# Scatters, router gathers and the last batch moved in the experts' block of a graph transformer layer

## The reference

```python
xn = layernorm(x)
x  = x + gnn(xn, edges) + linear_attention(xn)       # gnn: mean of xn[src] by dst, a matmul, a norm
x2 = layernorm(x)
h  = (x2 @ W_gat).reshape(M, 4, 4)                   # heads, experts
e  = leaky_relu(a_src[src] + a_dst[dst], 0.2)        # a_* = (h * att_*).sum(-1), one per head
alpha = exp(e - segment_max(e, dst)) / segment_sum(...)
agg = segment_sum(h[src] * alpha, dst) + b_gat
scores = layernorm(agg).reshape(M, 4, 4).mean(1)
gate = softmax of the best two scores, 0 for the others
out = x + sum over experts of gate * (gelu(x2 @ W1 + b1) @ W2 + b2)
```

## Time and profile before

| | us |
|---|---|
| Median of three timed runs | 4273.77 |
| Profiled execution, its span (no other time of it is given) | 5331.2 |
| Set-up, to the first gather | 130 |
| Graph block, first gather to last | 2511 |
| Graph block, what is left after the gathers | 192 |
| Experts' block, all tiles | 2128 |
| Experts' block, gates and sums | 370 |

### The profile page before, as it was taken

The page is one execution under the profiler, slowest core; times in us unless marked ns, Lnnn a source line. Parts: engine busy times, 40 slices in busy tenths (PEclk is TensorE's granted clock), DMA queues, the critical chain, the costliest instruction groups (busy, mean ns, idle before and its releaser), DMA issues. The chain is left out here.

```text
span 5331.2 us, 46344 instructions
## 1 busy us (share of the span) xinstructions
PE 3564.3 (67%) x12937; PEld 2313.0 (43%) x12938; DVE 2082.9 (39%) x4892; ACT 801.1 (15%) x1970; POOL 2832.6 (53%) x2937
## 2 busy tenths in 40 slices
PE   0688888888757777777626377768685777789200
PEld 0455555555445455555413154444453454455100
DVE  5456655665546555544311020211111120212378
ACT  5111211111101111111101011111111111112000
POOL 2666666666666666666655623653636444630420
PEclk9889899998878888888767588888787788899655
DMA  7444444444445555555512111211112111211387
GB/s 250 128 109 115 112 111 112 112 115 112 112 111 148 138 153 154 162 152 152 125 33 61 18 49 28 58 38 48 35 50 43 44 48 36 60 50 48 118 254 253
DMA packets 381413, 540.57 MB, mean 101 GB/s; under 512 B 120314, under 2 KB 297818, under 8 KB 381143
## 3 DMA queue, kind: packets, MB, share of 16 engines
q0 software_dynamic: 119136, 234.44, 20.0%
q1 hardware_dynamic: 243119, 288.12, 16.8%
q10 hardware_dynamic: 19016, 16.48, 0.9%
HBM read 392.03 MB, written 146.74 MB: 101 GB/s over the span
## 5 line engine op out<-in xcount | busy, mean ns | idle before, releaser
L788 POOL DMA_INDIRECT rows<-xn_rows,gsrc x1664 | 1606.6, 965 | 908.5 <-issue 459.8
L1357 POOL DMA_INDIRECT nb<-route_rows,idx x1024 | 1000.3, 977 | 897.7 <-DVE msg L1432 480.9
L1093 PE MATMUL PS<-rows,oh 128*128 128x257 f32 x3328 | 910.0, 427 | 351.9 <-issue 220.0
L1686 PE MATMUL PS<-arena,hid 128*125 128x256 f32 x3200 | 865.1, 422 | 408.5 <-issue 298.6
L1686 PEld LDWEIGHTS PS<-arena,hid 128*125 128x125 f32 x3200 | 662.9, 209 | 621.3 <-issue 502.6
L1093 PEld LDWEIGHTS PS<-rows,oh 128*128 128x128 f32 x3328 | 693.8, 214 | 488.8 <-issue 296.6
L1621 DVE TENSOR_TENSOR y_sb<-PS,b_b 125x512 f32<-125x512 f32 x200 | 128.7, 685 | 1781.4 <-remote 975.2
L1678 PE MATMUL PS<-x2g,arena 128*128 128x500 f32 x1600 | 722.6, 610 | 147.3 <-issue 94.0
L1678 PEld LDWEIGHTS PS<-x2g,arena 128*128 128x128 f32 x1600 | 313.5, 197 | 541.6 <-issue 473.0
L1647 ACT ACTIVATE hid<-PS,b_sb 128x500 f32<-128x500 f32 x400 | 269.9, 677 | 1109.9 <-PE PS L1678 688.9
L1165 PE MATMUL PS<-own_w,p_t 128*125 128x512 f32 x400 | 231.2, 662 | 77.7 <-ACT s_t L1053 54.5
(11 more groups left out here) (304 smaller groups left out, 3086.8 us busy)
## 6 DMA issues: line engine op xcount, KB each, us to landing
y_rows<-y_sb SPq DMA_DIRECT2D x100, 512.0 KB
arena<-y_rows SPq DMA_DIRECT2D x100, 512.0 KB
rows<-xn_rows,gsrc POOLq DMA_INDIRECT x1664
nb<-route_rows,idx POOLq DMA_INDIRECT x1024
sum_rows<-kept SPq DMA_DIRECT2D x104, 128.5 KB
x_rows<-x SPq DMA_DIRECT2D x100, 128.0 KB
hid<-x_rows SPq DMA_DIRECT2D x100, 128.0 KB
m_in<-sum_rows SPq DMA_DIRECT2D x100, 125.5 KB
```

The lines of the kernel that those rows point to most:

```text
L788: pool.indirect_dma_start(out=rows[w][h][:, q, 0:D], out_offset=None, in_=xn_rows, in_offset=bass.IndirectOffsetOnAxis(ap=gsrc[:, s * HU + ...
L1093: last = mm(SUM[:, 0:D + 1], oh[w][h][:, q, :], rows[w][h][:, q, :], start=h == 0 and q == 0, stop=h == 1 and q == HU - 1)
L1357: pool.indirect_dma_start(out=nb[b % NBUF][:, c, :], out_offset=None, in_=route_rows, in_offset=bass.IndirectOffsetOnAxis(ap=idx[:, b * W ...
L1686: last = mm(Y[j % 2][e // 2][0:NP, (e % 2) * D:(e % 2 + 1) * D], hid[:, 4 * e + k, j * NP:(j + 1) * NP], w2_sb[:, e, k, :], start=k == 0, ...
```

## The change

The hundred scatters leave the graph block and stand at the head of GpSimd's queue in the experts' block, without waits. `start_ad`'s load moves in SyncE's queue from ahead of all tiles to behind the store of tile 6. The full stops (REST) go; the wait for the gather four before stays. The batches stand behind tiles 12, 20, 24, 32, 36, 41, 48, 53, 60, 65, 72, 76, 84, 88 and 96, and batch 15 (`LATE`) behind all tiles, on VectorE, ScalarE and SyncE. The joining of the lanes follows it, and TensorE's transposes for it stand behind its last tile.

```diff
 def unit_after(b):
-    t = int((b + 1) * 5.65) + 3
+    t = int((b + 1) * 5.8) + 7
     return t if t % 4 < 2 else t + 4 - t % 4
...
 # graph block, gpsimd
-                for t in range(NT):
-                    pool.wait_ge(s_hc, t + 2)
-                    pool.indirect_dma_start(out=ad_rows, out_offset=bass.IndirectOffsetOnAxis(ap=start_i[:, t:t + 1], axis=0),
-                                            in_=ad_all[:, t, :], in_offset=None).then_inc(s_ads, 16)
...
 # experts' block
-            LAST = unit_after(NB - 1)
+            LATE = [b for b in range(NB) if unit_after(b) > NT - 4]
...
 # sync
+                def store_records(b):
+                    sp.wait_ge(s_rec, b + 1)
+                    sp.dma_start(rec_rows[0:EF, :].rearrange("(p f) c -> p f c", p=P)[:, b * W:(b + 1) * W, :],
+                                 rec[b % 2][:]).then_inc(s_recs[b % 2], 16)
                 load_group(0)
                 load_group(1)
-                sp.wait_ge(s_ads, 16 * NT)
-                sp.dma_start(ad[:], ad_rows[0:EF, :].rearrange("(p f) h -> p f h", p=P)).then_inc(s_adl, 16)
                 for t in range(NT):
                     sp.wait_ge(s_yc, t + 1)
                     sp.dma_start(y_rows[t], y_sb[t % 2][:]).then_inc(s_ys[t % 2], 16)
+                    if t == unit_after(0) - 6:
+                        sp.wait_ge(s_ads, 16 * NT)
+                        sp.dma_start(ad[:], ad_rows[0:EF, :].rearrange("(p f) h -> p f h", p=P)).then_inc(s_adl, 16)
                     for b in batches_after(t - 2):
-                        sp.wait_ge(s_rec, b + 1)
...
+                        store_records(b)
...
                 for t in range(YR):
                     final_loads(t)
+                for b in LATE:
+                    store_records(b)
                 for t in range(YR, NT):
                     final_loads(t)
 # gpsimd
+                for t in range(NT):
+                    pool.indirect_dma_start(out=ad_rows, out_offset=bass.IndirectOffsetOnAxis(ap=start_i[:, t:t + 1], axis=0),
+                                            in_=ad_all[:, t, :], in_offset=None).then_inc(s_ads, 16)
                 for b in range(NB):
                     if b >= NBUF:
                         pool.wait_ge(s_nbf, b - NBUF + 1)
                     for c in range(W):
-                        if (b or c) and c % REST == 0:
-                            for q in range(AHEAD):
-                                pool.wait_ge(s_nb[q], (b * W + c) // AHEAD * 16)
-                        elif b or c >= AHEAD:
+                        if b or c >= AHEAD:
                             pool.wait_ge(s_nb[c % AHEAD], (b * W + c) // AHEAD * 16)
 # vector, behind the loop over tiles
-                    for part, at in ((lane_ends, 1), (over_lanes, 2), (lane_sums, 3), (first_maxima, 4), (first_records, 5)):
-                        if t == LAST + at:
-                            part()
+                for b in LATE:
+                    scores(b)
+                    records(b)
+                for part in (lane_ends, over_lanes, lane_sums, first_maxima, first_records):
+                    part()
 # scalar, behind the loop over groups
-                    if g == LAST // 4:
-                        act.wait_ge(s_endd, 1)
-                        a(dc[:], dc[:], ACT.Exp).then_inc(s_ende, 1)
+                for b in LATE:
+                    act.wait_ge(s_dif, b + 1)
+                    a(dd[:], dd[:], ACT.Exp).then_inc(s_ex, 1)
+                act.wait_ge(s_endd, 1)
+                a(dc[:], dc[:], ACT.Exp).then_inc(s_ende, 1)
 # tensor: the waits and transposes of the lanes' ends (before, inside group() behind tiles LAST + 2 and
 # LAST + 3) stand, unchanged and in the same order, behind the last group
```

More of the change, by code:

```diff
@@ L50 @@
 AHEAD = 4
-REST = 16
 EVEN = 112
@@ L1287, in build @@
             batches_after = lambda t: [b for b in range(NB) if unit_after(b) == t]
-            LAST = unit_after(NB - 1)
-            assert LAST + 4 < NT and LAST // 4 == NG - 2
+            LATE = [b for b in range(NB) if unit_after(b) > NT - 4]
             @block.sync
@@ L1310, in _ @@
                     sp.dma_start(y_rows[t], y_sb[t % 2][:]).then_inc(s_ys[t % 2], 16)
+                    if t == unit_after(0) - 6:
+                        sp.wait_ge(s_ads, 16 * NT)
+                        sp.dma_start(ad[:], ad_rows[0:EF, :].rearrange("(p f) h -> p f h", p=P)).then_inc(s_adl, 16)
                     for b in batches_after(t - 2):
-                        sp.wait_ge(s_rec, b + 1)
-                        sp.dma_start(rec_rows[0:EF, :].rearrange("(p f) c -> p f c", p=P)[:, b * W:(b + 1) * W, :],
-                                     rec[b % 2][:]).then_inc(s_recs[b % 2], 16)
+                        store_records(b)
                     if t % 4 == 0 and t // 4 + 2 < NG:
@@ L1688, in group @@
                         last.then_inc(s_y, 1)
[L1689 to L1698, removed]
                 for g in range(2):
@@ L1706, in _ @@
                     group(g, g % 2, g // 2)
+                pe.wait_ge(s_ends, 1)
+                for k in range(4):
+                    last = nc.tensor.transpose(HP[0][0:20, k * P:(k + 1) * P], ends[:, k, :], ident)
+                last.then_inc(s_endt, 1)
+                pe.wait_ge(s_endc, 1)
+                pe.wait_ge(s_fx, 1)
+                nc.tensor.transpose(HP[1][:, 0:20], fm[:, 0:P], ident[0:20, 0:20])
+                nc.tensor.transpose(HP[1][:, 20:40], fx[:, 0:P], ident[0:20, 0:20]).then_inc(s_back, 1)
 _INS = ["x", "src", "dst", "L0_gnn_weight", "L0_gnn_bias", "L0_mix_Wqkv", "kv_turned", "out_turned", "L0_mix_bout",
```

## The result

The kernel after takes **4129.98 us** (median of four runs, 4125.64 to 4134.59) against 4273.77: a ratio of **0.9667** [0.9655, 0.9679], 3.3% or 144 us less. Forecast were 4184 us (2.1%) and a range of 4113 to 4305. The side was right, the size was not.

The account below looks back on a forecast made before the run. GpSimd was taken to set the graph block's step, and the experts' loop in timed runs; in the profile it alternated with TensorE. Profile -110 + 0 + 32 = -78 and timed -77 - 30 = -107 gave -90: 4184 us, range 4113 to 4305.

Parts of the forecast that it names:

- Post steps: Graph block's end: twelve or thirteen steps remain after the last gather, 4.6 us each, 60 us, plus some 8 for last sums.
- timed view: Sum for a run without most of TensorE's slowdown: graph tail -77 us, experts' block 1494 to 1464, together -107.
- profile's -110: Graph block, by the 5331.2 us profile: without scatters its last step ends near 2710 for 2820.25 us.
- Scatters at the head: Start of the experts' block: 100 scatters of 1.27 us add 127 us to GpSimd; SyncE's wait taken as 0.
- Full stops: Router's gathers: 63 stops, 13 on a wait for `records`, the other 50 cost 2.3 us each; removal saves GpSimd 113 us.
- Loop over tiles: 0: Experts' block, in the profile's terms: the loop of about 2128 us does not change.
- The chain of the last batch: End of the experts' block: 57 us from the last tile to the weighing against 25 before, +32 us.
- The final sum: Whole kernel: -78 us by the profile, -107 in a timed run, forecast -90, giving 4184 us.
- Stops as relief: Rival, experts' block: stops relieve TensorE, so without them it crawls more; slower, 4347 us, chance 0.13.
- Timed runs bound by TensorE: Rival, experts' block: the stops hid nothing, only -45 us stays; 4229 us, chance 0.20.
- A tail at 12 us: Rival, graph block's end: steps keep their 12 us pace, no change; 4270 us, chance 0.11.
- Stops in another form: Rival, router's gathers: the wait for the gather four before stops GpSimd as often; +26 us, 4300 us, chance 0.06.

Follow-up runs that it names:

- e4: The kernel after with all scatters put back behind the graph block's gathers: 4157.49 us, ratio 0.9735.
- e2: The kernel before without its full stops, nothing else changed: 4140.01 us, ratio 0.9686.
- e5: The kernel before with a full stop at every 8th gather in place of every 16th: 4387.1 us, ratio 1.0276.
- e3: The kernel after with the full stops put back: 4271.99 us, ratio 0.9996.
- e6: The kernel after with the batches and the joining of the lanes at their old places, start_ad's load behind tile 4's store: 4184.46 us, ratio 0.9799.
- e8: The kernel after with a VectorE drain behind every fourth of the 20 scans of `records`: 4098.61 us, ratio 0.9595.

## Why the prediction was right in its direction and short in its size

- **Post steps, "13 x 4.6 = 60 us".** The product came near by luck, since neither the number of steps nor their pace held. In after ten steps end behind the last graph gather, the first copy at 2251.39 and the last at 2302.96 us, so 51.57 / 9 = 5.7 us apart and 56 us behind that gather (2246.7); GpSimd's idle time at the block's end is 57.8, so the 8 us of last sums that were added to the 60 did not show. The timed view's -77 measured -79.3. The profile's -110 was from the crawl: in an undisturbed run the post steps were done at 2298 us beside the scatters, and it was the scatters themselves, to 2375, that kept the block open.
- **Scatters at the head, +127.** Right: 127.5. SyncE's wait behind tile 6 cost nothing, as taken: the load of `ad` was issued at 2435.77, and over the whole block TensorE waited for VectorE's tiles once, 8.3 us.
- **Full stops, "13 fall on a wait for `records`; over the other 50 it is 2.3 us each".** This step failed, and it is the largest miss. The size of one was right (2.2), but an undisturbed run has no wait for `records`, so all 63 count: -139 of idle time and -133 from first to last gather, for -113. The 480.9 us on which the 13 rested were a mark of the crawl, which made VectorE late.
- **"Loop over tiles: 0".** It fell with the crawl. The timed view had the block as 1494 to 1464; it measured 1577.6 to 1518.8 (first gather or scatter to weighing), -58.8 for -30. Of the 29 us too few, 20 are the stops, and 9 the end: 108.1 to 54.9 us from the last gather to the weighing, for 101 to 57.
- **The chain of the last batch, 57 us.** Right in length (54.9), wrong in its start. It hangs on the last gather and not on the last tile, which came 38.5 us earlier; from that tile to the weighing it was 93.4 us, one of the text's own signs of being wrong. Where the tiles do come last, in e4, it was 60.8. "Last gather at 1407 with its tiles done at about 1385" left 22. A gather's mean pitch was 1336.4 / 1023 = 1.31 us and not 1.25, as some are held up (last section).
- **The final sum.** The timed view gave -107; with the measured stops and end it is -107 - 20 - 9 - 2 = -138, the difference of the two spans (the medians give -144). Taking -90 between it and -78 cost another 17. The text had noted a span 1057 us over the median, and found the crawl likelier to be the profile's; to lean on that profile for half of the sum was the second failing step. Both of its terms came out otherwise (-79.3 for -110, -58.8 for 0 + 32).
- **Rivals.** *Stops as relief* fell in e2 and e5. *Timed runs bound by TensorE* fell: the stops cost nearly their full time there. It comes close only once the stops are gone (e2). *A tail at 12 us* fell with steps 5.7 us apart. *Stops in another form* fell: all waits for the gather four before are 18.7 us in after (30 of them), with gathers landing 2.4 us after issue in the median.
- **What the sum of parts hides.** Stops alone are -132 (e2), everything else alone 0 (e3), both -144. Within "everything else" the gains don't add. The scatter move is worth 27.5 beside the new places (after against e4) and costs 44 without them (e6 against e2). The places are worth 54 beside the scatter move (e6 against after) and cost 17 without it (e4 against e2). The scatter move takes time from the block's start and gives it to GpSimd's line; the places decide how many tiles stand behind GpSimd's last gather. Each was worth something only beside the other.

## What to carry to other kernels

Hold a profile's span against the timed median before anything is read from it: where they differ by a quarter, a second profile of the same kernel is worth more than any argument from the first. A full stop in a queue of transfers cost 1.8 to 2.2 us here, near the 2.4 us in which a gather lands, every time it was passed; count none as covered unless a trace that matches the timed runs shows the wait that covers it. When two engines run a stage side by side, look at what the engine that needs both waits for, and at how much work is queued behind that wait. The last starts tell which is late only where nothing is queued behind them. Work that can go on either side of a stage's border (here the scatters) can be split until neither engine waits for the other.

## What the runs showed that was not expected

**VectorE's runs of scans hold up GpSimd's gathers.** VectorE's and GpSimd's timelines of the same microseconds, of after:

```profile
2695.56 1.70 DVE L1432 TENSOR_TENSOR msg<-nb,dd 128x320 f32<-128x320 f32 x4
2697.35 5.32 DVE L1436 TENSOR_TENSOR_SCAN rec<-dd,rec,msg 128x64 f32<-128x64 f32 x20
```

```profile
2698.83 1.00 POOL L1357 DMA_INDIRECT nb<-route_rows,idx  x1 [0.30 <-issue]
2700.13 3.34 POOL L1357 DMA_INDIRECT nb<-route_rows,idx  x1 [0.30 <-issue]
2703.78 0.94 POOL L1357 DMA_INDIRECT nb<-route_rows,idx  x1 [0.30 <-issue]
```

A gather takes 0.94 us. The one that starts 1.5 us into the scans still passes in 1.00, the next takes 3.34 and ends 0.8 us after them. Fifteen gathers of after take over 2.5 us each, one in each batch of scans but the last, which has no gathers beside it, 34 us above the usual in all. In e8, with the same scans and four drains among them, none does. Over the same kind of stretch, of e8:

```profile
2692.20 6.09 DVE L1438 TENSOR_TENSOR_SCAN rec<-dd,rec,msg 128x64 f32<-128x64 f32 x20
```

```profile
2693.67 0.94 POOL L1357 DMA_INDIRECT nb<-route_rows,idx  x1 [0.30 <-issue]
2694.92 0.94 POOL L1357 DMA_INDIRECT nb<-route_rows,idx  x1 [0.30 <-issue]
2696.17 0.94 POOL L1357 DMA_INDIRECT nb<-route_rows,idx  x1 [0.30 <-issue]
```

The scans take 0.8 us more, the gathers nothing. The Trainium skill (SBUF — State Buffer, Who interferes with whom) says that a VectorE instruction with two SBUF inputs contends with a GpSimd instruction that reads SBUF, and that copies, casts and scalar operations in their two-port modes can lock it out. The section names scans in neither of its lists, but a scan of `dd` and `msg` has two SBUF inputs. The four TENSOR_TENSOR of L1432 have them too, and the four gathers of after that they lengthen, to 1.25 to 1.27 us, end within 0.02 us of them. So this trace agrees with the first statement in both forms, though not every gather beside the scans is held. That gaps in the run of scans set the gathers free is shown; which port or lock it is was not tried.

**One execution in which TensorE crawled.** The same kernel had a span of 5331.2 us once and 4271.2 us the next time, with TensorE at 0.66 and at 3.5 records a us beside gathers. No other profile of this study shows it, with stops or without. Its cause is open.
